# A ternary layer's first product: from fp32 passes to three bf16 parts of the input

## The reference, cut to what matters

```
def _ternary_weight(w, group_size):            # group_size 64
    wb = w.astype(bfloat16); wg = wb.reshape(-1, group_size)
    scale = clip(mean(abs(wg), -1), 1e-8)      # one scale per 64 weights, bf16
    q = clip(round(wg / scale), -1, 1)         # -1, 0 or 1
    qs = (q * scale).reshape(w.shape).astype(w.dtype)
    return w + stop_gradient(qs - w)

w1 = _ternary_weight(W_fc, 64)                 # 1024 x 256
h  = square(relu(x @ w1.T))
hn = h * rsqrt(mean(square(h), -1) + eps)
out = hn @ _ternary_weight(W_proj, 64).T       # 256 x 1024
```

## Time and profile before

| | |
|---|---|
| runs (us) | 1836.72, 1841.16, 1840.79: median 1840.79 |
| the profiled execution's own time | 1839.08 us |
| its span | 1837.0 us |
| TensorE clock granted, mean over the span | 0.956 of full |
| end of the mixer | about 1004 to 1072 us of the span |
| ternary layer | about 1072 to 1207 us |

### The profile page before, as it was taken

One profiled execution on the slowest core, in us unless ns is written; L12 is line 12 of the kernel. 1 busy time (PEld: TensorE's weight loads), 2 busy tenths in 40 slices (PEclk: granted clock), 3 DMA queues, 4 the chain that ended last, 5 costly groups with the idle time before them and its releaser, 6 DMA issues.

```text
span 1837.0 us, 25324 instructions
## 1 busy us (share of the span) xinstructions
PE 1669.1 (91%) x9852; PEld 987.9 (54%) x9852; DVE 996.3 (54%) x1703; ACT 772.9 (42%) x1789; POOL 406.7 (22%) x473
## 2 busy tenths in 40 slices
PE   7999788989999999689997988977999999989998
PEld 4666443434333335445554546754777777764556
DVE  4666665667787771352444853315666676741222
ACT  2422245657767776322111121126566666642110
POOL 2321001011110000220000058504444444540000
PEclk9999688989999999889998999988999999999999
DMA  5000120000000002010000030000000020000000
GB/s 169 3 7 18 52 70 2 1 1 1 2 1 2 1 2 97 0 48 0 0 1 15 1 115 1 0 6 1 7 1 7 1 78 1 1 1 0 12 12 23
DMA packets 28360, 34.96 MB, mean 19 GB/s; under 512 B 5713, under 2 KB 24722, under 8 KB 27730
## 3 DMA queue, kind: packets, MB, share of 16 engines
q1 hardware_dynamic: 28242, 33.35, 5.8%
HBM read 23.74 MB, written 2.10 MB: 14 GB/s over the span
## 4 chain that ended last, share of the span: by engine, by line
PE 71%; DVE 12%; POOL 7%; issue 6%; ACT 3%; DMA 0%; SPq 0%; POOLq 0%; DVEq 0%; ACTq 0%
PE PS L1159 7%; PE PS L1405 6%; PE PS L1146 6%; PE PS L1411 6%; PE PS L1121 6%; PE PS L1426 5%; PE PS L2244 3%; PE PS L2233 2%; PE PS L1907 2%; DVE arena L1351 2%; PE PS L2211 2%; PE PS L1890 2%; PE PS L339 2%; POOL arena L2429 2%; PE PS L2186 2%
## 5 line engine op out<-in xcount | busy, mean ns | idle before, releaser
L1351 DVE TENSOR_REDUCE arena<-PS 128x1 f32<-128x1024 f32 (+7 forms) x320 | 329.9, 1061 | 133.5 <-PE PS L1123 96.0
L1257 ACT ACTIVATE arena<-PS 128x512 f32<-128x512 f32 (+3 forms) x640 | 318.0, 533 | 162.0 <-PE PS L1149 74.8
L1146 PE MATMUL PS<-arena 99*128 99x512 bf16 (+3 forms) x640 | 208.4, 357 | 1.6 <-ACT arena L1257 1.0
L1121 PE MATMUL PS<-arena 96*128 96x512 bf16 (+3 forms) x640 | 182.6, 364 | 14.2 <-DVE arena L1351 13.5
L190 POOL TENSOR_TENSOR rstd<-ve,mhalf 128x4 f32<-128x4 f32 x32 | 32.3, 1010 | 599.7 <-DVE ve L218 599.7
L1159 PE MATMUL PS<-arena 128*32 128x512 f32 (+3 forms) x1280 | 154.8, 556 | 2.8 <-ACT arena L1263 1.7
L185 ACT ACTIVATE XT<-PS 128x1024 f32<-128x1024 f32 x32 | 32.8, 1024 | 273.4 <-PE PS L178 273.4
L1146 PEld LDWEIGHTS PS<-arena 99*128 99x128 bf16 x640 | 61.1, 100 | 153.4 <-ACT arena L1257 112.7
L1405 PE MATMUL PS<-XT,arena 128*128 128x512 f32 x256 | 122.7, 602 | 5.6 <-DVE R L200 3.5
L2244 PE MATMUL PS<-arena 128*128 128x256 f32 x512 | 121.0, 379 | 2.0 <-DVE R L200 2.0
L1411 PE MATMUL PS<-XT,arena 128*128 128x512 f32 x256 | 120.3, 592 | 0.0
(11 more groups left out here) (242 smaller groups left out, 2857.7 us busy)
## 6 DMA issues: line engine op xcount, KB each, us to landing
arena<-arena SPq DMA_DIRECT2D x55, 128.0 KB, 2.4
XT<-in_L_attn_xT SPq DMA_DIRECT2D x4, 512.0 KB, 6.7
X<-in_L_attn_x SPq DMA_DIRECT2D x4, 512.0 KB, 9.4
arena<-in_L_attn_out_w SPq DMA_DIRECT2D x1, 2048.0 KB, 7.3
out<-X SPq DMA_DIRECT2D x4, 512.0 KB, 2.9
arena<-in_dmask SPq DMA_DIRECT2D x1, 1024.0 KB, 5.7
arena<-in_L_ffn_W_up SPq DMA_DIRECT2D x1, 1024.0 KB, 5.8
arena<-in_L_ffn_W_gate SPq DMA_DIRECT2D x1, 1024.0 KB, 7.9
```

The source lines that it names most:

```text
L1121: last = pe.matmul(flat[:, o:o + w], q, a.KS[0:SROWS, CH * kc:CH * kc + w], start=True, stop=kc < c)
L1146: last = pe.matmul(PS[:, b, lo:CH], a.KS[0:rows, P * j:P * (j + 1)], a.QS[0:rows, G1 * g + r, CH * c + lo:CH * (c + 1)], start=True, stop= ...
L1257: act.activation(a.PB[:, n % 3, r, lo:CH], PS[:, 4 + x % 3, lo:CH], ACT.Exp, scale=D0 ** -0.5).then_inc(a.e2, 1)
L1351: dve.tensor_reduce(dst, src, AX.X, ALU.max, negate=True).then_inc(a.m1, 1)
```

## The change

The first product of the ternary layer takes bf16 operands. The weight: DVE's step 2 writes scale x sign in bf16 over the sign buffer `a.wb[0]`, which becomes `a.up`, and the steps 3 and 4 (minus w, plus w) are left out for the first weight. `TERNARY_DVE` lists the 6 + 10 steps, so the second weight's begin four steps earlier. The input: each chunk of `XT` is split into three bf16 parts in `a.XP`. ScalarE copies it to bf16 (`x_high`), DVE subtracts that (`x_residual`, into the fp32 buffer `a.xr`, of which there is one), ScalarE copies the rest to bf16 (`x_middle`), DVE subtracts again and writes bf16 (`x_low`). `up` then makes 2 x 3 bf16 products for each group and waits for `x_low` of its chunk.

Where the split stands in the streams: ScalarE in the mixer, `x_high(0)` behind the XT copy of chunk 0, `x_middle(0)`, `x_high(1)` behind that of chunk 1, `x_middle(1)`, `x_high(2)` behind that of chunk 2, `x_middle(2)`, `x_high(3)` behind that of chunk 3; in the ternary layer `x_middle(3)` behind the 8 relus of chunk 0. DVE in the mixer, behind `tail_dve` of chunk 1 `x_residual(0)`, of chunk 2 `x_low(0)`, `x_residual(1)`, of chunk 3 `x_low(1)`, `x_residual(2)`; in the ternary layer `x_low(2)`, `x_residual(3)` behind `hidden(0)`, and `x_low(3)` behind `hidden(1)`.

```diff
@@ -1696,9 +1696,16 @@
         if c >= 2:
             act.wait_ge(a.conv, c)
             tail_act(k, act, NC * 5 + c - 2, c - 2)
+            act.wait_ge(k.xt_done, NC * 4 + c - 1)
+            if c >= 3:
+                x_middle(k, act, c - 3)
+            x_high(k, act, c - 2)
     act.wait_ge(a.conv, NC)
     for c in (NC - 2, NC - 1):
         tail_act(k, act, NC * 5 + c, c)
+        act.wait_ge(k.xt_done, NC * 4 + c + 1)
+        x_middle(k, act, c - 1)
+        x_high(k, act, c)
 
 
 def l2_pool(k, pool, st):
@@ -1750,6 +1757,10 @@
         if c + 1 < NC:
             front(c + 1)
         tail_dve(k, dve, st, NC * 4 + c, c)
+        if c >= 2:
+            x_low(k, dve, c - 2)
+        if c >= 1:
+            x_residual(k, dve, c - 1)
 
 
 
@@ -1771,7 +1782,9 @@
     a.acc = v(14 * n + 1536, [P, 2, CH])
     a.rs = v(14 * n + 2560, [P, NT])
     a.g64 = v(14 * n + 2576, [P, P])
-    a.up = a.q[:, 0, :].rearrange("p (t e) -> p t e", t=KT)
+    a.up = a.wb[0].rearrange("p (t e) -> p t e", t=KT)
+    a.XP = v(0, [P, NC, 3, KT, CH], BF16)
+    a.xr = v(4 * n, [P, KT, CH])
     a.down = a.q[:, 1, :].rearrange("p (t e) -> p t e", t=HT)
     a.ld = k.sem("l2f_ld")
     a.wb_s = k.sem("l2f_wb_s")
@@ -1786,11 +1799,13 @@
     a.ssq = k.sem("l2f_ssq")
     a.ms = k.sem("l2f_ms")
     a.rms = k.sem("l2f_rms")
+    a.x_cast, a.x_res, a.x_low = k.sem("l2f_x_cast"), k.sem("l2f_x_residual"), k.sem("l2f_x_low")
 
 
 HALF2 = KT * HID // 2
 TERNARY_ACT = {(0, 2): (0, 0, 0), (0, 3): (0, 0, 1), (0, 4): (0, 1, 0), (0, 5): (0, 1, 1), (0, 6): (0, 2, 0), (0, 7): (0, 2, 1),
                (1, 0): (1, 0, 0), (1, 1): (1, 0, 1), (1, 6): (1, 1, 0), (1, 7): (1, 1, 1), (2, 0): (1, 2, 0), (2, 1): (1, 2, 1)}
+TERNARY_DVE = [(0, step, half) for step in range(3) for half in range(2)] + [(1, step, half) for step in range(5) for half in range(2)]
 
 
 def ternary_sp(k, sp, I):
@@ -1849,9 +1864,9 @@
         dve.tensor_scalar(a.sc[m][:, CH * n:CH * (n + 1)], k.PS[:, T_BANK + n % 2, :], 1.0 / 64, 1e-8, ALU.mult,
                           ALU.max).then_inc(a.sc_s, 1)
     p = HT * (c - 1) + it - 4
-    m, step, half = p // 10, p % 10 // 2, p % 2
-    if not 0 <= m < 2:
+    if not 0 <= p < len(TERNARY_DVE):
         return
+    m, step, half = TERNARY_DVE[p]
     cols = slice(HALF2 * half, HALF2 * (half + 1))
     q, w, sc, sign = a.q[:, m, cols], a.w[:, m, cols], a.sc[m][:, cols], a.wb[m][:, cols]
     if step == 0:
@@ -1864,7 +1879,7 @@
         last = dve.tensor_tensor(q, q, sc, ALU.mult)
     elif step == 2:
         dve.wait_ge(a.wb_s, 4 * m + 2 + half + 1)
-        last = dve.tensor_tensor(q, q, sign, ALU.mult)
+        last = dve.tensor_tensor(sign if m == 0 else q, q, sign, ALU.mult)
     elif step == 3:
         last = dve.tensor_tensor(q, q, w, ALU.subtract)
     else:
@@ -1876,19 +1891,49 @@
     pass
 
 
+def x_high(k, act, c):
+    a = k.l2f
+    act.activation(a.XP[:, c, 0, :, :], k.XT[:, :, CH * c:CH * (c + 1)], ACT.Copy).then_inc(a.x_cast, 1)
+
+
+def x_middle(k, act, c):
+    a = k.l2f
+    act.wait_ge(a.x_res, c + 1)
+    act.activation(a.XP[:, c, 1, :, :], a.xr, ACT.Copy).then_inc(a.x_cast, 1)
+
+
+def x_residual(k, dve, c):
+    a = k.l2f
+    dve.wait_ge(a.x_cast, X_HIGH[c])
+    if c >= 1:
+        dve.wait_ge(a.x_low, c)
+    dve.tensor_tensor(a.xr, k.XT[:, :, CH * c:CH * (c + 1)], a.XP[:, c, 0, :, :], ALU.subtract).then_inc(a.x_res, 1)
+
+
+def x_low(k, dve, c):
+    a = k.l2f
+    dve.wait_ge(a.x_cast, X_MIDDLE[c])
+    dve.wait_ge(a.x_res, c + 1)
+    dve.tensor_tensor(a.XP[:, c, 2, :, :], a.xr, a.XP[:, c, 1, :, :], ALU.subtract).then_inc(a.x_low, 1)
+
+
+X_HIGH, X_MIDDLE = (1, 3, 5, 7), (2, 4, 6, 8)
+
+
 def l2f_pe(k, pe):
     a, PS = k.l2f, k.PS
-    pe.wait_ge(a.part, 20)
+    pe.wait_ge(a.part, len(TERNARY_DVE))
 
     def up(c):
-        pe.wait_ge(k.xt_done, NC * 4 + c + 1)
+        pe.wait_ge(a.x_low, c + 1)
         for it in range(HT):
             n = HT * c + it
             if n >= 2:
                 pe.wait_ge(a.r_s, n - 1)
             for kt in range(KT):
-                last = pe.matmul(PS[:, n % 2, :], a.up[:, kt, P * it:P * (it + 1)], k.XT[:, kt, CH * c:CH * (c + 1)],
-                                 start=kt == 0, stop=kt == KT - 1)
+                for part in range(3):
+                    last = pe.matmul(PS[:, n % 2, :], a.up[:, kt, P * it:P * (it + 1)], a.XP[:, c, part, kt, :],
+                                     start=(kt, part) == (0, 0), stop=(kt, part) == (KT - 1, 2))
             last.then_inc(a.mm, 1)
 
     def main(c):
@@ -1921,6 +1966,8 @@
             if n >= 2:
                 act.wait_ge(a.h_s, n - 1)
             act.activation(a.r[:, n % 2, :], k.PS[:, n % 2, :], ACT.Relu).then_inc(a.r_s, 1)
+        if c == 0:
+            x_middle(k, act, NC - 1)
         if c >= 2:
             tail_act(k, act, NC * 6 + c - 2, c - 2)
     for c in (NC - 2, NC - 1):
@@ -1969,9 +2016,13 @@
             dve.tensor_tensor(a.h[:, c % 2, it, :], r, r, ALU.mult).then_inc(a.h_s, 1)
 
     hidden(0)
+    x_low(k, dve, NC - 2)
+    x_residual(k, dve, NC - 1)
     for c in range(NC):
         if c + 1 < NC:
             hidden(c + 1)
+        if c == 0:
+            x_low(k, dve, NC - 1)
         dve.wait_ge(a.ssq, c + 1)
         dve.tensor_scalar(a.rs[:, TPC * c:TPC * (c + 1)], PS[:, 3, 0:TPC], 1.0 / HID, EPS_F32, ALU.mult, ALU.add)\
            .then_inc(a.ms, 1)
```

## The result

The kernel after takes 1844.0 us (median of 17 runs, 1839.15 to 1849.41), the one before 1839.43 us (median of 17). The ratio is 1.003, with a 95% interval of 1.0018 to 1.0043: slower by 0.3%, 3.3 to 7.9 us. The profiled execution took 1843.6 us with a span of 1841.6 us, 4.6 us longer than before.

A forecast was written before the change was run, and what follows sets the result against it. POOL's sums of squares and power were taken to hold the ternary layer's first half and be late next behind a faster product. +1.9 + 2.6 - 2.7 - 1.3 = +0.5 us gave 1841.3 us; range 1836.5 to 1845.5.

The forecast's parts named there:

- DVE's two operations in layer 2: End of layer 2, behind chunk 2: x_low(0) and x_residual(1) take 2.53 us against 1.11 us idle, +1.42 us.
- entry of POOL's chain behind L200: Start of the ternary layer: ScalarE's copies delay the relus; POOL starts +1.9 us later, 1.7 of it from layer 2.
- three DVE operations against POOL: Ternary layer: x_low(2), x_residual(3), x_low(3) each lengthen POOL's sums of squares by 0.86 us, +2.6 us together.
- L203 of chunk 0 to 1: Ternary layer: TensorE would release this sum 3.4 us earlier, POOL only 2.72, so the interval shrinks by 2.7 us.
- L203 of chunk 1 to 2: Ternary layer: POOL's power ends at 1183.04 and becomes what is late, so the interval shrinks by only 1.3 us.
- L203 of chunk 2 to 3: Ternary layer's last interval: the last chunk has no up, so nothing is gained.
- if TensorE still releases L203: Sign of a wrong forecast: the sums of chunks 1 and 2 should be released by POOL's power L1954, not TensorE.
- The 3.4 us themselves: First ternary product: a group takes 1.29 instead of 1.72 us, saving 3.4 us per chunk.
- the rival on the clock: TensorE waits longer ahead of the last chunk; its second product loses 1.7 us to half clock: 1843.0 us, chance 0.15.
- If a stage outside these two moves: Sign of a wrong forecast: only the end of layer 2 and the ternary layer should change.
- The cover of the layer before: Layer before: TensorE hides the removed and earlier DVE weight steps; without that cover 4.9 us to gain.
- The slower rival: First product: weight loads of 0.10 us don't hide, a group takes 1.89 us: +7.3 us, 1848.1 us, chance 0.06.

The follow-up runs named there:

- the split alone: Kernel before plus only the three-part split; first product stays fp32 but waits for the split: 1840.87 us, ratio 1.0014 to before.
- the product alone: Kernel after without middle and low parts; all six bf16 passes per group take the high part: 1836.89 us, ratio 0.9984 to before.
- the power early: Kernel after with POOL's power of each chunk moved into the middle of the next chunk's squares: 1833.93 us, ratio 0.9957 to before.
- The eight passes: Kernel after plus eight unread bf16 passes in TensorE's wait ahead of the ternary layer's last chunk: 1838.08 us, ratio 0.9990 to before.
- the fp32 kernel with the power early: Kernel before with POOL's power moved into the middle of the next chunk's squares: 1831.83 us, on a second run 1832.30 us.

## Why the prediction was right, and which steps were not

The time, 1844.0 us, lay in the range, in part by luck. The forecast added 0.5 us to a median of three runs, 1840.79 us; the median of 17 is 1839.43, and the measured difference is 4.6 us. Counted from 1839.43 the range would have ended at 1844.1. Its ratio's interval, 0.18 to 0.43%, holds the line of 0.3%, so that "no difference" and "slightly slower" are not told apart. The mechanism, a saving that POOL turns away and a split that is paid on the chain, is shown by the split alone, the product alone and the power early. But the sum was +0.5 us, and the two profiles give +5.7 us from the cut on. Nearly all of what is missing is TensorE's clock, 1.7 us in the last chunk and 3.6 us in layer 3, which the sum held at nothing. Step by step:

| step | forecast | profile |
|---|---|---|
| DVE's two operations in layer 2 | +1.42 | +1.41 |
| DVE's operation behind chunk 1 (ahead of the cut) | +0.27 | +0.16 |
| entry of POOL's chain behind L200 | +0.2 | +0.34 |
| three DVE operations against POOL | +2.6 | +2.33 |
| L203 of chunk 0 to 1 | -2.7 | -2.22 |
| L203 of chunk 1 to 2 | -1.3 | -1.46 |
| L203 of chunk 2 to 3 | 0 | +1.68 |
| layer 3 | 0 | +3.6 |

- **The additions beside POOL.** Right to 0.3 us: 0.86 us for an operation of 1.22. The prediction read the rule of the Trainium skill ("SBUF — State Buffer", Who interferes with whom), exclusion for the whole instruction, as 3.7 us in all. The trace bears the exclusion out, with DVE's 2.06 to 2.28 us. It does not bear out that price: DVE's turn begins while POOL is between two operations, and POOL pays only the part that is left.
- **The entry.** Right in size, wrong in reason. I wrote that the second relu follows at once and POOL hardly waits. TensorE still ran at half clock (0.50 granted from 1074 to 1077), the second relu came 1.43 us behind the first, and POOL idled 0.69 us for it as before. Two errors of some 0.5 us cancelled, and that is luck.
- **Chunk 1.** The step that failed: "TensorE would release it 3.4 us earlier, POOL 2.72". It took over the cold start of `up(2)` as it was, 1.7 us. After, `up(2)` ran at half clock up to 1132 and took 13.05 us in the chain for 47 of its 48 passes; the record of the first is missing and lies in the 0.45 us of "issue" ahead, so it was some 13.4 us, 3.1 over the 10.35 of 48 passes at 0.2156. So TensorE and not POOL released L203, 0.6 us later than POOL would have (1152.93 + 1.02, against 1154.61). The prediction named "if TensorE still releases L203" as a sign of being wrong, and for this chunk it came.
- **The 3.4 us themselves** were too much. From L203 of chunk 1 to the sum over partitions TensorE needs 15.55 us before and 12.88 after, 2.7 us less: the passes are as cheap as forecast, but in the middle of `up` TensorE waits 0.62 us for a relu (0.71 with the power early), which no step had. Even with POOL out of the way the product gives 2.6 us per chunk and not 3.4.
- **The last chunk.** The forecast gave it nothing; the rival on the clock, with 0.15, named the place and 1.7 us, and it came with 1.68. I had argued that the wait is shorter than the one seen. It was 2.15 us, and that was enough. The eight passes show that this wait did it. The chance was too small.
- **Layer 3.** "If a stage outside these two moves" stood among what would make the forecast wrong. It moved, by 3.6 us, and no rival had it. That is the larger part of what was missing, and it is clock as well.
- **The cover of the layer before** held: the XT copies of its first three chunks stand 1.34 to 1.35 us earlier in the profile after, as the four copies ahead of them do, that of its last chunk 1.53. The ternary steps there gained at most 0.2 us.
- **The slower rival**, exposed weight loads, is refuted by 24 passes in 5.35 us.

## What to carry to other kernels

Before a product is made cheaper, follow the chain to see who holds the next step: here a 1 us instruction of POOL, queued behind 20 us of squares, was worth 6 to 8 us, and the cheaper product with its split nothing until it was moved. Price the preparation of a cheaper operand by where its instructions stand in their queues: with the power early, L203 of chunk 0 came 4.8 to 5.5 us later behind the cut than in the fp32 kernel as they were placed, and 1.2 to 1.8 us later a few places on. And a faster TensorE that then waits is not merely idle: it can come back at half clock, also in a layer behind.

## What the runs showed that I had not expected

- A wait of TensorE of 2.15 us was followed by half clock over some 3 us of the next product (15.62 instead of 13.94 us); eight passes for nothing in it avoided that and, with it, 4.1 us in layer 3. The length of the wait alone does not set the price: behind the same 2.15 us the product alone lost 3.0 us (16.96 instead of 13.94).
- What the clock costs can repeat: stretch and rest of the kernel after repeated to 0.04 us in two profiles (144.10 and 144.12, 639.42 and 639.45), while the executions differed by 5.6 us in the layers 0 and 1. It need not: the fp32 kernel with the power early differed by 0.6 and 0.4 us.
- DVE and POOL take turns: beside POOL a DVE operation of 1.23 us lasts 2.06 to 2.28 us, and POOL's next operation 0.86 us more, which is less than the DVE operation's own length.
